# One layer on one core: experts on lists of the tokens that chose them, in place of every expert on every token

## The chip, the core and the metric

The kernel runs on one core of a Trainium2 chip. Its engines are TensorE (PE; PEld is its weight load), the vector engine (DVE), ScalarE (ACT), GpSimd (POOL) and SyncE (SP), which issues most transfers. Transfers between DRAM and the on-chip SBUF run on 16 DMA engines. The metric is device time in microseconds (us) of one execution; lower is better.

## What is computed

One layer on 4096 tokens of 256 features: a layer norm, causal attention with 16 heads of 16 features, a residual, a second norm, and a mixture of experts with a shared part. The expert part of the reference, cut:

```python
scores = sigmoid(xf @ gate_w.T); sfc = scores + gate_bias      # 16 experts in 4 groups
masked = where(in one of the 2 best groups, sfc, -inf)
_, topk_idx = top_k(masked, 4)                                  # 4 experts per token
topk_w = 2.5 * scores[topk_idx] / sum(scores[topk_idx])
cw = one_hot(topk_idx, 16) weighted by topk_w                   # 0 for the other 12
hg = einsum('nh,eih->nei', xf, Wg); hu = einsum('nh,eih->nei', xf, Wu)
y = einsum('nei,ne,ehi->nh', silu(hg) * hu, cw, Wd)             # i = 128
y = y + silu(xf @ Ws_g.T) * (xf @ Ws_u.T) @ Ws_d.T              # shared, 256 wide = 2 units
out = x + gb * (h + y)                                          # h: the normed input xf
```

Twelve of a token's sixteen expert weights `cw` are zero.

## The kernel before

All stages work on blocks of 512 tokens (8 blocks, `NB`). Every block of code ends in a barrier of all engines, after which the SBUF of its temporaries is given to the next.

- **prepare** (to 103 us): norm, transposes, queries, keys and values; parts of queries and keys go through DRAM.
- **attend** (to 1672 us): a list of events (`attention_order`) sets the order on every engine. POOL clears the triangle of each diagonal step (L628), and at 8 places adds the bias to a block of x (L618), which SP loads and stores (L606, L609).
- **project** (to 1777 us): a pipeline of 14 steps over the blocks. Per block PE projects the attention's result, DVE adds the residual (L980), takes statistics and normalises (L999), POOL raises to the power -0.5 (L942), PE transposes, ACT applies the modulation per feature and writes h2 (L914). A router chain on DVE (`router`, some 50 short instructions per two blocks) is threaded between. It makes `cw`, which goes to DRAM. Beside it SP loads the 18 units' weights (16 experts and the shared part as two units), ACT rounds each to float32r (`whi`, L909) and POOL takes the remainder (`wlo`, L945).
- **experts** (to 2404 us): each of the 8 blocks passes through all 18 units. A unit is 12 matmuls up (L1256: gate and up, two halves of the features, three products of high and low parts) and 6 matmuls down (L1267), all with 512 moving columns. ACT takes the silu (L1292) and the high part of the product (L1295), DVE multiplies by the up part (L1332), by `cw` (L1338) and takes the low part (L1345). The sum over the units stays in PSUM. Per block it is then scaled, turned back (L1278), added to x1 (L1363) and stored (L1233).

## Time and profile before

| | us |
|---|---|
| median of 3 runs | 2396.38 (2381.59 to 2401.0) |
| the profiled execution, its own time | 2405.99 |
| its span in the profile | 2404.3 |
| mean granted clock of TensorE, share of full | 0.947 |

The span is what the instructions cover; the execution's own time lies 1.7 us above it. A busy time is the time in which an engine executed; matmuls overlap, so the busy share of PE says less than the spacing of its instructions. An arrow names what the waiting instruction was released by.

### The profile page before, as it was taken

Reading aid. Unit: us, or ns where it says so; the run is one execution under the profiler, and the core shown is the slowest. Engines: PE = TensorE matmul, PEld = TensorE weight load, DVE = VectorE, ACT = ScalarE, POOL = GpSimd, SP = SyncE. Lnnn points to the kernel's source line nnn. Section 1 sums busy time; section 2 is a strip of 40 time slices with the busy share of each in tenths; the row PEclk is TensorE's granted clock in tenths of the full one; section 3 lists DMA queues with packets and bytes.
Section 4 is the critical chain, followed back from the end, with each engine's and each line's share of the span. In section 5 each row is a group of like instructions: output and inputs, shape, how many; then the busy total and the mean of one; then the engine's idle time right before and its main releaser. Section 6 shows DMA issues by size and latency. Waiting matters only on the chain. (4 is left out here: it accounts for less than half of the span.)

```text
span 2404.3 us, 42528 instructions
## 1 busy us (share of the span) xinstructions
PE 2245.1 (93%) x17842; PEld 1218.8 (51%) x17842; DVE 1756.9 (73%) x2243; ACT 1464.7 (61%) x2831; POOL 154.4 (6%) x191
## 2 busy tenths in 40 slices
PE   7689999999999999999999999998869999999998
PEld 5233333343444444444444333333758878788786
DVE  6478879999998878999998887762765555455554
ACT  5136657788888877788888888875523333333332
POOL 2000000000000011100000000000600000000000
PEclk9758969999999999999999999997969999999999
DMA  7715000004000003300000000001522221122211
GB/s 229 222 27 67 17 16 17 1 25 62 25 2 17 24 17 63 50 17 17 17 17 8 2 8 8 2 2 55 185 73 70 71 70 61 61 87 70 70 62 36
DMA packets 59907, 117.01 MB, mean 49 GB/s; under 512 B 7313, under 2 KB 20882, under 8 KB 58962
## 3 DMA queue, kind: packets, MB, share of 16 engines
q1 hardware_dynamic: 57168, 109.73, 16.7%
q10 hardware_dynamic: 2562, 4.77, 0.5%
q8 instruction: 129, 2.11, 0.4%
q14 instruction: 48, 0.39, 0.1%
HBM read 84.46 MB, written 29.62 MB: 47 GB/s over the span
## 5 line engine op out<-in xcount | busy, mean ns | idle before, releaser
L737 DVE TENSOR_REDUCE mx<-S 128x2 f32<-128x1024 f32 (+3 forms) x1152 | 1279.2, 1134 | 208.4 <-PE S L650 135.5
L718 ACT ACTIVATE prob<-ST 128x512 f32<-128x512 f32 (+3 forms) x2304 | 1168.6, 559 | 361.3 <-PE ST L671 316.5
L685 PE MATMUL O<-prob,V 128*17 128x256 f32 (+1 forms) x8704 | 691.0, 391 | 0.2 <-POOL prob L628 0.2
L650 PE MATMUL S<-K,Q 48*128 48x512 f32 (+3 forms) x2304 | 572.3, 495 | 33.0 <-DVE mx L737 23.1
L671 PE MATMUL ST<-Q,K 49*128 49x512 f32 (+3 forms) x2304 | 493.6, 425 | 36.3 <-ACT prob L718 30.7
L650 PEld LDWEIGHTS S<-K,Q 48*128 48x128 f32 x2304 | 224.5, 192 | 475.7 <-issue 293.5
L671 PEld LDWEIGHTS ST<-Q,K 49*128 49x128 f32 x2304 | 225.0, 191 | 138.3 <-ACT prob L718 105.7
L685 PEld LDWEIGHTS O<-prob,V 128*17 128x17 f32 x8704 | 145.7, 96 | 289.6 <-issue 280.3
L1295 ACT ACTIVATE ahi<-pr 128x512 fp32r<-128x512 f32 x144 | 91.1, 632 | 206.9 <-DVE pr L1338 194.8
L1292 ACT ACTIVATE sg<-hg 128x512 f32<-128x512 f32 x144 | 86.1, 598 | 209.2 <-PE hu L1256 208.5
L1332 DVE TENSOR_TENSOR sg<-sg,hu 128x512 f32<-128x512 f32 x128 | 88.0, 687 | 161.9 <-ACT sg L1292 161.3
L628 POOL TENSOR_SCALAR_AFFINE_SELECT prob<-prob 128x512 f32<-128x512 f32 x128 | 81.2, 635 | 1530.5 <-ACT prob L718 1530.5
L1345 DVE TENSOR_TENSOR alo<-pr,ahi 128x512 fp32r<-128x512 f32 x144 | 99.6, 692 | 100.5 <-ACT ahi L1295 100.5
L1267 PE MATMUL ya<-ahi,whi 128*128 128x512 f32 x288 | 113.3, 394 | 10.5 <-DVE alo L1345 10.5
L1256 PE MATMUL hg<-hhi,whi 128*128 128x512 f32 x288 | 114.0, 396 | 7.1 <-DVE hlo L1352 4.4
L1256 PE MATMUL hg<-hlo,whi 128*128 128x512 f32 x288 | 112.7, 391 | 0.0
L1256 PE MATMUL hg<-hhi,wlo 128*128 128x512 f32 x288 | 112.6, 391 | 0.0
L1256 PE MATMUL hu<-hhi,whi 128*128 128x512 f32 x288 | 112.5, 391 | 0.0
L1256 PE MATMUL hu<-hlo,whi 128*128 128x512 f32 x288 | 112.5, 391 | 0.0
L1256 PE MATMUL hu<-hhi,wlo 128*128 128x512 f32 x288 | 112.5, 391 | 0.0
L1267 PE MATMUL ya<-alo,whi 128*128 128x512 f32 x288 | 112.2, 389 | 0.0
L1267 PE MATMUL ya<-ahi,wlo 128*128 128x512 f32 x288 | 112.1, 389 | 0.0
(150 smaller groups left out, 1436.7 us busy)
## 6 DMA issues: line engine op xcount, KB each, us to landing
cwb<-cw SPq DMA_DIRECT2D x32, 1024.0 KB, 5.6
Q<-qs SPq DMA_DIRECT2D x192, 64.0 KB, 2.4
K<-ks SPq DMA_DIRECT2D x18, 512.0 KB, 15.3
qs<-hl SPq DMA_DIRECT2D x16, 512.0 KB, 4.4
ks<-hl SPq DMA_DIRECT2D x16, 512.0 KB, 4.2
wraw<-in_wcat SPq DMA_DIRECT2D x18, 384.0 KB, 3.4
xin<-in_x SPq DMA_DIRECT2D x4, 1024.0 KB, 12.5
xgate<-in_x SPq DMA_DIRECT2D x8, 512.0 KB, 3.8
```

The source lines that it names most:

```text
L628: pool.affine_select(out=tri, in_=tri, compare_op=ALU.is_ge, fill=0.0, base=0, pattern=[[0, HG], [1, P]], channel_multiplier=-1).then_inc( ...
L650: ins = pe.matmul(out[:, ab, 0:w], Q[g, n % QR, p, r * P:(r + 1) * P], K[G % 2][g, p, c * BW:c * BW + w], start=True, stop=not diag)
L671: pe.matmul(ST[(u + ab) % ST_BANKS][:, c0:BW], K[G % 2][g, p, k * P:(k + 1) * P], Q[g, n % QR, p, c0:BW], start=True, stop=True).then_inc( ...
L685: ins = pe.matmul(O[32 * a:32 * a + VC, c0:c1], V[:, G, k, VC * a:VC * (a + 1)], prob[:, s % NP, a, c0:c1], start=s in FIRST and h == 0, s ...
L718: act.activation(prob[:, s % NP, 2 * p + ab, c0:BW], ST[u % ST_BANKS][:, c0:BW], ACT.Exp).then_inc(s_exp, 1)
L737: dve.tensor_reduce(mx[:, n % 2, a:a + step + 1:step, c], S[slot % S_RING][:, :, 0:w], AX_X, ALU.max).then_inc(s_free, 1)
L1256: ins = pe.matmul(bank[:, :], w[:, u, c0:c0 + I], h[:, p, half, :], start=(m == 0), stop=(m == 5))
L1267: ins = pe.matmul(ya[p][:, half, :], w[:, u, c0:c0 + P], a[:, i, :], start=(u == 0 and m == 0), stop=(u == U - 1 and m == 2))
L1292: act.activation(sg[:, i, :], hg[i][:, :], ACT.Silu).then_inc(q["silu"], 1)
L1295: act.activation(ahi[:, i, :], pr[:, i, :], ACT.Copy).then_inc(q["ahi_done"], 1)
L1332: dve.tensor_tensor(sg[:, i, :], sg[:, i, :], hu[i][:, :], ALU.mult).then_inc(q["dve_chain"], 1)
L1345: dve.tensor_tensor(alo[:, i, :], pr[:, i, :], ahi[:, i, :], ALU.subtract).then_inc(q["act_full"], 1)
```

## The change

Each expert now gets a list of the tokens that chose it, in DRAM, and works on tiles of 512 rows of its list. The number of tiles is fixed at 47, which is (4096 x 4 + 16 x 511) / 512 rounded down, enough for any division of the tokens over the experts; which expert and which row a tile has is computed by the kernel and read into registers.

- **prepare**: the modulation of the second norm and the gate `gb` are made as rows spread over all partitions (`modB`, `gbB`), by four matmuls of 512 and 256 columns and DVE instructions of 128x256.
- **attend**: the bias of x leaves. In its place the weights are split: 54 pieces of 128x256 (3 per unit) are loaded (WL), on POOL rounded and the remainder taken, a third of them first scaled by `gbB` (WP), and both parts stored to DRAM (WS).
- **project**: x is loaded straight from the input, 6 blocks at first and 2 later, and POOL adds the bias (L953). DVE makes the modulated row h in two passes per tile of 128 tokens, into `xe`, which holds 256 features, the 16 weights and the token's number (273 columns). SP loads the split weights. After the router of two blocks, PE counts for every token and expert the earlier ones that chose it (`places`), DVE makes from it the row of the list (`placing`), and at the end `tiles` makes the tables of the tiles. POOL sends the first half of the 128 row groups to the lists (`scatter`).
- **experts**: POOL sends the other half. Meanwhile SP writes empty rows behind each list, clears the accumulator `acc1`, and the shared part runs on the 8 blocks with x1 and h added, into `acc0`. Then the 47 tiles: load the 512 rows, pick the weight of the tile's expert, turn, multiply up, multiply down with the tokens as output rows, scale by the weight, and add each 128 rows to `acc0` or `acc1` at their tokens' numbers (L1366 in the changed kernel). Last, `acc0` + `acc1` is the output.

The core of the diff:

```diff
+XW = D + E + 1
+CAP = T + BW
+NTILES = (T * TOPK + E * (BW - 1)) // BW
+SC_SPLIT = 2
+CWR = 4
+XR = 6
@@ attend, POOL
-                    if kind == "XS":
-                        need("xl", s_xl, 16 * (e + 1))
-                        pool.tensor_tensor(xg[:, :, :], xg[:, :, :], ...
+                    if kind == "WP":
+                        need("wl", s_wl, 16 * (e + 1))
+                        need("ws", s_ws, 32 * e)
+                        if e % 3 == 2:
+                            pool.tensor_tensor(wraw[:, :], wraw[:, :], t["gbB"][:, :], ALU.mult).then_inc(s_wp, 1)
+                            need("wp", s_wp, 3 * e + 1)
+                        pool.tensor_copy(wcut[:, 0, :], wraw[:, :]).then_inc(s_wp, 1 + (e % 3 < 2))
+                        need("wp", s_wp, 3 * e + 2)
+                        pool.tensor_tensor(wcut[:, 1, :], wraw[:, :], wcut[:, 0, :], ALU.subtract).then_inc(s_wp, 1)
@@ project, DVE
+                    for i in range(TPB):
+                        h = xe[:, TPB * b + i, 0:D]
+                        dve.scalar_tensor_tensor(out=h, in0=x_of(b)[:, i, :], scalar=mv[:, b % 2, i, 0:1],
+                                                 in1=t["modB"][:, 1, :], op0=ALU.subtract,
+                                                 op1=ALU.mult).then_inc(s_xm, 1)
+                        route(2)
...
+                        dve.scalar_tensor_tensor(out=h, in0=h, scalar=rstd[:, b % 2, i:i + 1],
+                                                 in1=t["modB"][:, 0, :], op0=ALU.mult, op1=ALU.add).then_inc(s_xn, 1)
@@ project, POOL, behind the last power(b)
+                for g in range(SC_SPLIT):
+                    pool.wait_ge(s_idx, g + 1)
+                    scatter(pool, t, d, g)
...
+def scatter(pool, t, d, g):
+    for n in range(2 * TPB * g, 2 * TPB * (g + 1)):
+        for k in range(TOPK):
+            pool.indirect_dma_start(d["lists"], bass.IndirectOffsetOnAxis(ap=t["rows"][:, n, k:k + 1], axis=0),
+                                    t["xe"][:, n, :], None).then_inc(t["s_sent"], 16)
@@ experts, SP
+                for b in range(2):
+                    load_block(b, x1(b))
+                need("pad", s_pad, 2)
...
+                for e in range(E):
+                    row = sp.value_load(t["pad_row"][0:1, e:e + 1], min_val=0, max_val=E * CAP)
+                    sp.dma_start(d["lists"][bass.ds(row, BW), :].rearrange("(i p) c -> p i c", p=P), fill
+                                 ).then_inc(s_pads, 16)
...
+                sp.dma_start(d["acc1"].rearrange("(i p) c -> p i c", p=P),
+                             pad[:, 0:D].unsqueeze(1).broadcast_to([P, NT + 1, D])).then_inc(s_pads, 16)
+                for b in range(NB):
+                    need("yb", s_yb, b + 1)
+                    sp.dma_start(rows_of(d["acc0"], b), xb[:, b % 2, :, :]).then_inc(s_xo[b % 2], 16)
+                    if b + 2 < NB:
+                        load_block(b + 2, x1(b + 2))
+                need("pads", s_pads, 16 * (E + 3))
+                need("sent", t["s_sent"], 16 * NT * TOPK)
+                for r in range(NTILES):
+                    need(f"xo{r % 2}", s_xo[r % 2], 16 * NB // 2)
+                    load_tile(r)
@@ experts, POOL
+                for g in range(SC_SPLIT, 4):
+                    scatter(pool, t, d, g)
...
+                for r in range(NTILES):
+                    need("cwt", s_cwt, r + 1)
+                    for i in range(TPB):
+                        need("y", s_y, TPB * r + i + 1)
+                        need(f"add{i % 2}", s_add[i % 2], 16 * (TPB // 2 * r + i // 2))
+                        pool.indirect_dma_start(
+                            d[f"acc{i % 2}"], bass.IndirectOffsetOnAxis(ap=idt[:, r % CWR, i:i + 1], axis=0),
+                            yo[:, r % 2, i, :], None, compute_op=ALU.add).then_inc(s_add[i % 2], 16)
@@ experts, ACT: scale(q), one tile behind
+                        need("d", s_d, ends[q])
...
+                        for i in range(2):
+                            need(f"add{i}", s_add[i], 16 * TPB // 2 * (r - 1))
+                        for i in range(TPB):
+                            act.activation(yo[:, r % 2, i, :], y[:, i, :], ACT.Copy,
+                                           scale=cwt[:, r % CWR, i:i + 1]).then_inc(s_y, 1)
```

The order that the change makes, at three places. On PE, in the experts' stage, a unit of a block was this (`hg`, `hu`: gate and up, `ya`: down; the rows for the second half of the features read the same):

```order
L1256 MATMUL hu<-hhi,whi 128x512
L1256 MATMUL hu<-hlo,whi 128x512
L1256 MATMUL hu<-hhi,wlo 128x512
L1267 MATMUL ya<-ahi,whi 128x512
L1267 MATMUL ya<-alo,whi 128x512
L1267 MATMUL ya<-ahi,wlo 128x512
L1256 MATMUL hg<-hhi,whi 128x512
```

The same place is now, for a tile (`wst`: the unit's weights copied by DVE, `tpe`: the turned rows of the tile after next, `ye`: down, tokens as output rows):

```order
L1416 MATMUL hu<-hhi,wst 128x512
L1403 TENSOR_LOAD tile_unit
L1403 ISA x2
L1383 MATMUL tpe<-identf,xs 128x128 x8
L1431 ISA
L1431 MATMUL ye<-whi,ahi 128x256
L1431 MATMUL ye<-whi,alo 128x256
L1431 REGISTER_ALU
L1431 MATMUL ye<-wlo,ahi 128x256
```

Twelve matmuls up stay as they were, six of 512 columns down became twelve of 256, and eight transposes and a read of a register per tile are new.

On DVE a tile of the experts' stage now has these rows:

```order
L1548 TENSOR_TENSOR sg<-sg,hu 128x512
L1550 TENSOR_TENSOR alo<-sg,ahi 128x512
L1509 SCALAR_TENSOR_TENSOR pick<-expert,tile_e,xs 128x64
L1513 CAST idt<-xs 128x4
L1515 TENSOR_REDUCE cwt<-pick 128x4
L1520 TENSOR_LOAD tile_unit
L1520 ISA x2
L1522 ISA
L1522 COPY wst<-whi 128x512
L1522 REGISTER_ALU
L1522 COPY wst<-wlo 128x512
L1526 TENSOR_TENSOR hlo<-tpe,hhi 128x512 x2
```

The multiplication by `cw` over 128x512 has left the unit; the split of the input (`hlo`), once per block before, and two copies of weights are in every tile.

On POOL the last instructions of the projection and those of the experts' stage are now these (a row with x64 stands for 64 transfers of 128 rows each):

```order
L949 TENSOR_TENSOR rstd<-ve,half 128x4 x4
L1215 DMA lists<-big,rows 74240x273 x64
L863 UNCONDITIONAL_BRANCH
L1350 UNCONDITIONAL_BRANCH
L1353 MEMSET pad 128x273
L1355 TENSOR_SCALAR pad<-token 128x1
L1215 DMA lists<-big,rows 74240x273 x64
L1366 DMA acc<-yo,idt 4224x256 x188
```

POOL had no instruction in the experts' stage; it now issues 64 transfers before the barrier at the projection's end and 64 + 188 behind it.

## Rows read from the trace of the kernel before

**Rows 1.** head of the page: span, busy us (share) and instructions by engine

```profile
span 2404.3 us, 42528 instructions
PE 2245.1 (93%) x17842; PEld 1218.8 (51%) x17842; DVE 1756.9 (73%) x2243; ACT 1464.7 (61%) x2831; POOL 154.4 (6%) x191
```

**Rows 2.** stretches: length, busy us (count) by engine, clock, DMA share, GB/s

```profile
0.00:103.00 103.00, 68.10 (x302) 42.19 (x302) 52.65 (x156) 41.82 (x82) 13.51 (x28) 0.92 0.85 258
103.00:1672.00 1569.00, 1501.22 (x14497) 617.56 (x14497) 1312.20 (x1281) 1185.66 (x2337) 100.00 (x137) 0.95 0.10 21
1672.00:1777.00 105.00, 72.39 (x388) 64.54 (x388) 76.36 (x350) 37.83 (x59) 40.92 (x27) 0.74 0.45 153
1777.00:2404.00 627.00, 603.35 (x2656) 494.52 (x2656) 315.73 (x456) 199.36 (x353) 0.00 (x0) 0.99 0.20 67
```

**Rows 3.** groups, projection and experts: count | busy us, mean ns | idle before

```profile
L1256 PE MATMUL hg<-hhi,whi 128*128 128x512 f32 x288 | 114.0, 396 | 7.1 <-DVE hlo L1352 4.4 <-issue 2.6
L1267 PE MATMUL ya<-ahi,whi 128*128 128x512 f32 x288 | 113.3, 394 | 10.5 <-DVE alo L1345 10.5
...
L1345 DVE TENSOR_TENSOR alo<-pr,ahi 128x512 fp32r<-128x512 f32 x144 | 99.6, 692 | 100.5 <-ACT ahi L1295 100.5
L1295 ACT ACTIVATE ahi<-pr 128x512 fp32r<-128x512 f32 x144 | 91.1, 632 | 206.9 <-DVE pr L1338 194.8 <-DVE pr L1341 12.1
...
L1332 DVE TENSOR_TENSOR sg<-sg,hu 128x512 f32<-128x512 f32 x128 | 88.0, 687 | 161.9 <-ACT sg L1292 161.3
L1292 ACT ACTIVATE sg<-hg 128x512 f32<-128x512 f32 x144 | 86.1, 598 | 209.2 <-PE hu L1256 208.5
...
L999 DVE TENSOR_SCALAR xn<-xres,mv,rstd 128x256 f32<-128x256 f32 x32 | 14.9, 502 | 0.0
...
L1352 DVE TENSOR_TENSOR hlo<-h,hhi 128x512 fp32r<-128x512 f32 x16 | 10.3, 685 | 3.6 <-ACT hhi L1304 3.6
...
L1363 DVE TENSOR_TENSOR x1b<-x1b,ya 128x1024 f32<-128x1024 f32 x8 | 9.7, 1214 | 3.4 <-PE ya L1278 3.4
...
L1044 DVE MAX8 top<-sfc 128x8 f32<-128x16 f32 x32 | 2.8, 161 | 0.1
```

**Rows 4.** order of time on PE, projection: start us, us, what, idle before

```profile
1740.07 1.04 PE L1098 MATMUL tpx<-identf,xn 128*128 128x128 f32 x8
...
1740.94 1.86 PE L1109 MATMUL gl<-gwT,h 128*128 128x16 f32 x16
```

**Rows 5.** transfers: out<-in, queue, count, KB each, median us from issue to landing

```profile
Q<-qs SPq DMA_DIRECT2D x192, 64.0 KB, 2.4
...
x1b<-x SPq DMA_DIRECT2D x8, 512.0 KB, 6.7
out<-x1b SPq DMA_DIRECT2D x8, 512.0 KB, 3.1
...
cw<-cwT ACTq DMA_DIRECT2D x4, 64.0 KB, 1.5
```

**Rows 6.** GpSimd's instructions: ns min/median/max, first and last start, forms

```profile
L618 POOL TENSOR_TENSOR xgate<-xgate,gab x8: 2362/2373/2379, 344.9 to 1241.0; 128x1024 f32<-128x1024 f32 x8
L945 POOL TENSOR_TENSOR wlo<-wraw,whi x18: 1795/1810/1928, 1689.5 to 1748.5; 128x768 fp32r<-128x768 f32 x18
L942 POOL TENSOR_TENSOR rstd<-ve,half x8: 1018/1246/1258, 1688.5 to 1745.7; 128x4 f32<-128x4 f32 x8
```

**Rows 7.** order of time: DVE beside POOL, and the projection's end

```profile
1745.70 1.11 POOL L942 TENSOR_TENSOR rstd<-ve,half 128x4 f32<-128x4 f32 x1 [4.97 <-DVE ve L992]
...
1746.78 3.55 POOL L945 TENSOR_TENSOR wlo<-wraw,whi 128x768 fp32r<-128x768 f32 x2
1746.80 1.82 DVE L1039 TENSOR_SCALAR gtmp<-gtmp 128x32 f32<-128x32 f32 x1
1748.53 1.95 DVE L999 TENSOR_SCALAR xn<-xres,mv,rstd 128x256 f32<-128x256 f32 x1
...
1751.35 0.40 DVE L999 TENSOR_SCALAR xn<-xres,mv,rstd 128x256 f32<-128x256 f32 x1
...
1774.66 0.39 DVE L1056 TENSOR_TENSOR cwe<-sc,wsum 128x128 f32<-128x128 f32 x1
...
1775.92 0.34 ACTq L905 DMA_DIRECT2D cw<-cwT  x1
...
1780.00 0.29 PEld L1256 LDWEIGHTS hg<-hhi,whi 128*128 128x128 f32 x1 [4.71 <-DVE hlo L1352]
```

**Rows 8.** groups on the vector engine, first stage: copies from PSUM and from SBUF

```profile
L250 DVE COPY gtmp<-modp 1x256 f32<-1x256 f32 x1 | 0.4, 414 | 0.0
...
L252 DVE COPY grow<-gtmp 1x256 f32<-1x256 f32 x1 | 0.3, 281 | 0.0
```

**Rows 9.** who waited for whom: us in total, times, longest us

```profile
POOL prob L628 <- ACT prob L718: 1530.5, 128, 94.1
```

More of the change, by code:

```diff
@@ L923, in _ @@
                         turned(k)
[L924 to L926 removed]
                     if 0 <= k - 3 < NB:
[L928 removed]
+                        normed(k - 3)
                     if k >= 5 and k % 2 and (k - 5) // 2 < 4:
                         sigmoid((k - 5) // 2)
[L931 to L933 removed]
@@ L1282, in _, with turn @@
-                run(pe, section)
+                need = needs(pe)
+                units = {}
+                def turn(q):
+                    kind, x = jobs[q]
+                    if kind == "R":
+                        need(f"xs{x % 2}", s_xs[x % 2], 16 * (x // 2 + 1))
+                    need("lo", s_lo, NS * q)
+                    for half in range(NS):
+                        for i in range(TPB):
+                            rows = xe[:, TPB * x + i, :] if kind == "S" else xs[:, x % 2, i, :]
+                            ins = pe.transpose(tp[:, half, i * P:(i + 1) * P], rows[:, half * P:(half + 1) * P],
+                                               t["identf"][:, :])
+                        ins.then_inc(s_tp, 1)
@@ new lines, in pick_unit, with up @@
+                def pick_unit(q):
+                    kind, r = jobs[q]
+                    if kind == "R":
+                        units[q] = pe.value_load(t["tile_unit"][0:1, r:r + 1], min_val=0, max_val=E)
+                def up(it):
+                    q, u, first, last = items[it]
+                    if first:
+                        need("lo", s_lo, NS * (q + 1))
+                    if u is None:
+                        need("wst", s_wst, 2 * (jobs[q][1] + 1))
+                    for k, bank in ((0, hg[it % 2]), (1, hu[it % 2])):
+                        m = 0
+                        for half in range(NS):
+                            c0 = (k * NS + half) * I
+                            for part, h in ((0, hhi), (0, hlo), (1, hhi)):
+                                ins = pe.matmul(bank[:, :], up_weights(part, it, c0), h[:, q % 2, half, :],
+                                                start=(m == 0), stop=(m == 5))
+                                m += 1
+                    ins.then_inc(s_u, 1)
@@ new lines, in down @@
+                def down(it):
+                    q, u, first, last = items[it]
+                    need("act", s_act, it + 1)
+                    if first and q:
+                        if jobs[q - 1][0] == "R":
+                            need("y", s_y, TPB * tiles_before(q))
+                        else:
+                            need("yb", s_yb, blocks_before(q))
+                    for i in range(TPB):
+                        for m, (a, part) in enumerate(((ahi, 0), (alo, 0), (ahi, 1))):
+                            ins = pe.matmul(y[:, i, :], a[:, it % 2, i * P:(i + 1) * P],
+                                            down_weights(part, it), start=first and m == 0 and i % 2 == 0,
+                                            stop=last and m == 2, skip_group_check=True)
+                    ins.then_inc(s_d, 1)
@@ new lines, in _ @@
+                high(0)
+                high(1)
+                for it, (q, u, first, last) in enumerate(items):
+                    need("u", s_u, it + 1)
+                    need("act", s_act, it - 1)
+                    act.activation(sg[:, it % 2, :], hg[it % 2][:, :], ACT.Silu).then_inc(s_sg, 1)
+                    need("pr", s_pr, it + 1)
+                    if it >= 2:
+                        need("d", s_d, it - 1)
+                    act.activation(ahi[:, it % 2, :], sg[:, it % 2, :], ACT.Copy).then_inc(s_ahi, 1)
+                    if last:
+                        for ahead in turned_after(q):
+                            high(ahead)
+                    if it and items[it - 1][3]:
+                        scale(items[it - 1][0])
@@ L1369, in build @@
+                for b in range(NB):
+                    need(f"xb{b % 2}", s_xb[b % 2], 16 * (NB // 2 + b // 2 + 1))
+                    need(f"sum{b % 2}", s_sum[b % 2], 16 * (b // 2 + 1))
+                    dve.tensor_tensor(xb[:, b % 2, :, :], xb[:, b % 2, :, :], yo[:, b % 2, :, :],
+                                      ALU.add).then_inc(s_yb, 1)
 def build(nc, d):
```

737 lines of the change are left out of this document (413 added, 324 removed).

## The prediction

> **What bounds the kernel now.** I read the head of the page, then the busy time by stretch, then the groups of the last two stages. TensorE is busy 93% of the span [rows 1]. In the experts' stage it is busy 603 of 627 us at a clock of 0.99, with DVE at 316 and ACT at 199 [rows 2], and DVE and ACT wait for PE and for one another while PE hardly waits [rows 3]. The 2656 matmuls there are 8 x 18 x 18 = 2592 plus 64 transposes [rows 2]. At 0.13 us for a transpose (8 in 1.04 [rows 4]) the 64 take 8 us, so one 512-column matmul costs (603 - 8) / 2592 = 0.229 us. The projection has nobody at its limit: PE 72 and DVE 76 of 105 us, clock 0.74 [rows 2]. The transfers reach their highest use in the first stage: 258 GB/s at a share of 0.85 [rows 2]. POOL is nearly idle, 154 us in all [rows 1].
>
> **What the change takes away.** 144 units of 18 matmuls become 16 shared units and 47 tiles, 63 in all. If PE stayed the bound, the stage would lose more than half. So the question is what else sets the pace, part by part. Sums are against the span, 2404.
>
> *Prepare, +3.* Four matmuls and some 13 DVE instructions of 256 columns, 0.28 to 0.41 us each [rows 8], about 4 us; the transfers beside them hide a part. Bounds 0 and +5.
>
> *Attend, 0.* POOL gets 54 x 2 + 18 instructions of 256 columns. At 1810 ns for 768 columns [rows 6] that is 0.6 us each, 76 us, against 19 us removed (8 x 2373 ns). Before its triangles POOL idles 1530 us waiting for ACT [rows 9], and the pieces stand behind each block's diagonal steps, so the idle time covers them. Without that cover, one piece delays one triangle by 1.2 us: bounds 0 and +10.
>
> *Projection, +25.* DVE works 76 us here. Per block, four normalising instructions (502 ns mean [rows 3], part of it spent beside POOL, see below) become eight with two inputs, 0.41 each: +1.3 us, and +0.1 of wait. Times 8: +11. `placing` adds per two blocks three short instructions, eight MAX8 (161 ns [rows 3]) and a wait for nine matmuls, 2.8 us: +11. `tiles` is 15 chained instructions of up to 752 columns, at 0.7 us per 512 columns [rows 3] for the large ones: +6. POOL holds DVE up less (8 x 2.4 us in place of 18 x 1.8 [rows 6]): -3. Bounds +12 (idle DVE absorbs half) and +35.
>
> *The first half of the scatters, +32.* They stand behind the last rstd, which starts at 1745.7; the last transfer of the stage is issued at 1775.9 [rows 7], 30 us later; with the additions above, about 48 us. The barrier waits for POOL. 64 transfers of 128 rows with an index each are something this trace doesn't have. From below: an issue on ACT's queue, 0.34 us [rows 7], so 22 us and nothing shows. From above: POOL's smallest instruction (1.25 us for four columns [rows 6]) plus such an issue, 1.6 us, so 103 - 48 = +55. I take 1.25, what POOL needs to start and end anything with arithmetic: 80 - 48 = +32. The end of the stage, so far DVE's router, becomes POOL's.
>
> *Shared part, 130.* A block on PE: 2 x (12 x 0.229 + 12 down of 256 columns) + 8 transposes. For 256 columns the bounds are 0.116 us (16 matmuls of 16 columns with a full weight load each in 1.86 us [rows 4], or half of 0.229) and 0.229; I take 0.13, a transpose's. That gives 2 x (2.75 + 1.6) + 1.04 = 9.7 us. But the load of x1 for the third block stands on SP's queue behind 17 writes of 0.56 MB and 4.3 MB of zeros, 13.8 MB. At 258 GB/s that is 54 us, and the POOL scatters take a share of the same engines: 62 us, plus a landing of 6.7 [rows 5]. DVE waits there for x1, and PE behind it. Then six blocks at 9.7 to 10.5: store 3.1, load 6.7 [rows 5] and an addition of 1.2 [rows 3] just fit a block. 68 + 62 = 130; bounds 90 and 165. The second half of the scatters (80 us) lies inside.
>
> *First tile, 23.* The last block's store 3.1 and the load 6.7 [rows 5], DVE's part 5.7 (below), and some 7 for PE and ACT one after the other with nothing beside.
>
> *47 tiles, 7.0 us each.* Three things can set the pace.
> PE: 2.75 + 1.6 + 1.04 = 5.4 us; at 0.229 per 256 columns, 6.5.
> DVE: 0.69 + 0.69 + 2 x 0.685 [rows 3], two copies of 512 columns at about 0.42 (281 ns for 256 from SBUF [rows 8]), three small ones 0.6, a register read (not in the trace; 0 to 1, taken as 0.8), a wait of 0.7 for the high part: 5.7, so about 5.9 with seams.
> The adds: POOL issues four per tile, alternately to two accumulators, and each waits until the one before it to the same accumulator has landed. So a tile takes two full round trips A. An adding transfer with indices is nowhere in this trace. From below: a 64 KB write, 1.5 us [rows 5], A hidden. From above: a read trip of 2.4, a write trip of 1.5 [rows 5] and POOL's 1.25 us [rows 6] in series, 5.2. In between, read and write trip with one of the two issues counted: 2.4 + 1.5 - 0.4 = 3.5. I take this, since the add must read the row and write it, and the descriptors can be followed while POOL still makes them. 2 x 3.5 = 7.0 us, above the other two. 47 x 7.0 = 329.
>
> *Last sum, 55.* 8 x 1.5 MB at 258 GB/s is 49 us, plus a landing.
>
> Experts' stage: 3 + 130 + 23 + 329 + 55 = 540 against 627, **-87**. In all -87 + 3 + 25 + 32 = **-27: 2377**. The profiled execution took 1.7 us more than its span, and 2406 is 0.4% above the median, 2396.4; so 2379 x 0.996 = **2370**, 1.1% under the median.
>
> **A rule against the change.** While POOL subtracted weights for 3.55 us, two DVE instructions with SBUF operands took 1.82 and 1.95 us, one of which takes 0.40 alone [rows 7]: the two engines shut each other out. In every tile DVE copies weights from SBUF to SBUF twice, and here it is POOL that would be late. The Trainium skill (SBUF — State Buffer, "SBUF: two separate sides") says that descriptors of a POOL transfer can't be written while DVE runs a two-port copy. The rows agree that there is such a lock, but show it with POOL in front; what it would do is a rival below.
> The same skill (DMA: Bandwidth & Descriptors, "Anatomy of one DMA — SWDGE (gpsimd) path") fits some 2.0 us plus bytes / 436 GB/s for a POOL transfer; as an estimate from that page an add of 128 KB takes 2.3 us, no row shows one, and by it the adds would be hidden, which is the first rival.
>
> **Rivals.**
> *Adds hidden.* If A stays under 2.95 us, DVE sets 5.9 us a tile: 47 x 1.1 = 52 less, 2325, times 0.996 and the 1.7: 2318. For it: small transfers land in 1.5 and 2.4 us. Against: the add holds a read and a write in series.
> *Adds slow (slower than before).* One round trip on one accumulator decides. At A = 4.5 us a tile takes 9.0: +94, 2463. From A = 3.8 on the gain is gone (94 x 0.3 = 28). PE would then idle over 3 us per tile; in the projection, with PE at 69% busy, the clock was 0.74 [rows 2], and at the lower level a tile costs PE 10.8 us, so it can't recover much. For it: 5.2 is the upper bound, and POOL's start alone is 1.25 us.
> *Copies shut POOL out.* Each of two copies of 0.42 us, and what is queued with it, delays one add of the chain by up to 0.7: 8.4 us a tile, +66, 2435.
> *The way to the first tile is longer.* Scatters at 1.6 us (+23) and a shared part of 160 us (+30): 2423. For it: 23 MB in 90 us is what the engines did at their fullest.
>
> **How the numbers follow.** The likeliest case, A from 2.95 to 3.8, spans about 2318 to 2398 and has 0.36. Adds hidden 0.21, slow adds 0.25, copies 0.08, longer way 0.10. About 1% is what a measurement of this kernel can tell from no change. Faster by over 1% (below 2372): all of adds hidden and 0.20 of the likeliest, 0.41. Within 1%: 0.15 of the likeliest and 0.03 of the last two, 0.18. Slower: 0.41. The range, 2295 to 2490, cuts a tenth on either side: below, A hidden and a projection and shared part at their lower bounds; above, A at 4.8. The likeliest case's own range is 2318 to 2398.
>
> **What would show it.** On the page of the changed kernel: POOL's transfers of the first scatter at 1.25 us each and running about 32 us past DVE's last table; PE idle at the third shared block for some 40 us, released by DVE behind x1; then a steady period of 7.0 us in the tiles, ACT's scaling released by an add's landing, spacing of adds to one accumulator 3.5 us; PE 5.4 us busy per tile. Tiles of 5.9 us with DVE full would show the first rival, a spacing of 4 us or more the second, adds longer only beside the copies the third. It is wrong altogether if the attention gets longer, since all else rests on it keeping 1569 us.

## The result and the profile after

The changed kernel takes 2621.9 us (median of 4 runs, 2613.9 to 2630.6) against 2398.7 us before (4 runs): a ratio of 1.093, with a 95% interval from 1.084 to 1.102. It is 9% slower, and 132 us above the upper end of the range. The profiled execution took 2620.9 us, its span is 2619.2. Rows of before are those of the groups ahead of the prediction.

By stage, in the profile of the changed kernel (busy time by stretch; columns as in [rows 2]):

```profile
0.00:103.00 103.00, 68.73 (x286) 42.04 (x286) 54.81 (x157) 41.77 (x82) 13.29 (x27) 0.93 0.84 255
103.00:1667.00 1564.00, 1496.81 (x14496) 618.18 (x14496) 1312.46 (x1281) 1186.65 (x2337) 154.99 (x254) 0.95 0.13 29
1667.00:1862.00 195.00, 91.20 (x458) 82.22 (x458) 101.81 (x458) 20.10 (x37) 93.58 (x92) 0.63 0.45 164
1862.00:2028.00 166.00, 90.77 (x448) 72.97 (x448) 59.85 (x73) 29.42 (x49) 63.92 (x66) 0.75 0.67 186
2028.00:2557.00 529.00, 320.57 (x1504) 280.13 (x1504) 188.59 (x423) 183.99 (x376) 297.61 (x187) 0.80 0.56 97
2557.00:2619.00 62.00, 0.00 (x0) 0.00 (x0) 9.80 (x8) 0.00 (x0) 1.56 (x1) 0.50 0.68 207
```

The stretches are prepare, attend, the projection, the shared part, the tiles and the last sum. The attention ends at 1667 us, as before (1672, [rows 2]). PE works 320 us in the tiles' 529 us, at a clock of 0.80 where [rows 2] have 0.99. The whole distance to the forecast lies between 1667 and 2557.

| | forecast | first profile | e9, the same kernel again (chip 12) |
|---|---|---|---|
| prepare and attend | 1675 | 1667 | 1677 |
| projection with the first scatters | 162 | 195 | 170 |
| shared part, to the first tile's load | 133 | 166 | 154 |
| first tile and 47 tiles, to the last add's issue | 352 | 529 | 523 |
| last sum | 55 | 62 | 60 |
| span | 2377 | 2619 | 2584 |

Two things stand out. The tiles carry 177 us of the 242. And the two stages beside the scatters have something in the first profile that isn't there in e9: the other engines crawl (below).

**The tiles.** Groups of the page (line, out<-in, count, busy and mean ns, idle time before and what ended it), which answer to [rows 3] and [rows 9]:

```profile
L1366 POOL DMA_INDIRECT acc<-yo,idt x188 | 299.2, 1591 | 313.5 <-DMA acc<-yo,idt 149.9
L1383 PE MATMUL tpe<-identf,xs 128*128 128x128 f32 x376 | 79.5, 382 | 186.8 <-DVE hlo L1526 180.3
L1509 DVE SCALAR_TENSOR_TENSOR pick<-expert,tile_e,xs 128x64 f32<-128x64 f32 x47 | 13.3, 284 | 247.8 <-DMA acc<-yo,idt 242.6
L1488 ACT ACTIVATE ahi<-sg 128x512 fp32r<-128x512 f32 x63 | 39.7, 631 | 196.3 <-DVE sg L1548 195.5
L1215 POOL DMA_INDIRECT lists<-big,rows x128 | 125.5, 980 | 38.9 <-issue 38.9
```

DVE waits 243 us for landings of adds, PE and ACT wait for DVE. POOL's timeline in the steady state (start, us, what, idle before and its releaser):

```profile
2300.56 1.56 POOL L1366 DMA_INDIRECT acc<-yo,idt  x1 [3.37 <-DMA acc<-yo,idt]
2302.42 1.56 POOL L1366 DMA_INDIRECT acc<-yo,idt  x1 [0.30 <-issue]
2305.04 1.70 POOL L1366 DMA_INDIRECT acc<-yo,idt  x1 [1.06 <-DMA acc<-yo,idt]
2307.04 1.56 POOL L1366 DMA_INDIRECT acc<-yo,idt  x1 [0.30 <-issue]
2311.25 1.56 POOL L1366 DMA_INDIRECT acc<-yo,idt  x1 [2.65 <-DMA acc<-yo,idt]
```

Every second add goes to the same accumulator. From 2300.56 to 2305.04 a round trip takes 4.5 us, from 2305.04 to 2311.25 it takes 6.2. Two trips make a tile: 10.7 us, where the forecast had 2 x 3.5. The longer one starts 0.8 us ahead of a tile's load of 546 KB; SP's queue in the same stretch (two loads' issues merged into one row):

```profile
2305.87 11.11 SPq L1310 DMA_DIRECT2D xs<-lists  x2
```

**The scatters.** They are issued every 1.27 us (0.97 and 0.30 of issue), as forecast. But beside them the other engines crawl: each issues its next instruction late, although nothing that the profile shows holds it. It begins some 20 us after the first scatter (1749.4). DVE's router chain in the first profile:

```profile
1782.63 0.18 DVE L1056 TENSOR_TENSOR grank<-grank,gtmp 128x16 f32<-128x16 f32 x1 [1.22 <-DVE gtmp L1055]
1784.03 0.18 DVE L1057 TENSOR_TENSOR grank<-grank,gtmp 128x16 f32<-128x16 f32 x1 [1.22 <-issue]
1785.43 0.17 DVE L1055 TENSOR_TENSOR gtmp<-gs 128x8 f32<-128x8 f32 x1 [1.22 <-DVE grank L1057]
...
1805.77 0.09 DVE L1068 MEMSET top<- 128x32 f32 x1 [9.69 <-issue]
```

Instructions of 0.18 us come 1.40 us apart, and one comes 9.7 us late with nothing to wait for. After the scatters the same chain runs at 0.21 us a step. In the shared part it is PE's turn:

```profile
1919.31 0.37 PE L1383 MATMUL tpe<-identf,big 128*128 128x128 f32 x1 [2.21 <-issue]
1922.11 0.37 PE L1383 MATMUL tpe<-identf,big 128*128 128x128 f32 x1 [2.43 <-issue]
1924.91 0.37 PE L1383 MATMUL tpe<-identf,big 128*128 128x128 f32 x1 [2.43 <-issue]
```

Eight transposes, which take 1.04 us in [rows 4], come one per 2.80 us here.

One more thing differs between the two profiles of this kernel. The view of transfers gives the time from issue to landing where the landings are on record. It has none for the scatters of the first profile, and 3.7 us in e9:

```profile
lists<-big,rows POOLq DMA_INDIRECT x128
```

```profile
lists<-big,rows POOLq DMA_INDIRECT x128, 3.7
```

From the first scatter until 10 us behind the last, the trace of the first profile holds 350 records of landings, that of e9 2463.

### The profile page after: what moved, and what is told of

Read it like the earlier page. It is cut to its first block and busy times, and to the rows that moved or that the text cites. A ratio compares the mean times of both kernels' runs of the same rounds, so it can differ in the third digit from the quotient of the medians.

```text
span 2619.2 us, 43281 instructions
## 1 busy us (share of the span) xinstructions
PE 2068.1 (79%) x17192; PEld 1095.5 (42%) x17192; DVE 1727.3 (66%) x2398; ACT 1461.9 (56%) x2881; POOL 624.9 (24%) x627
## 5 line engine op out<-in xcount | busy, mean ns | idle before, releaser
L1366 POOL DMA_INDIRECT acc<-yo,idt x188 | 299.2, 1591 | 313.5 <-DMA acc<-yo,idt 149.9
L1383 PE MATMUL tpe<-identf,xs 128*128 128x128 f32 x376 | 79.5, 382 | 186.8 <-DVE hlo L1526 180.3
L1383 PEld LDWEIGHTS tpe<-identf,xs 128*128 128x128 f32 x376 | 63.7, 198 | 204.6 <-issue 195.7
L1215 POOL DMA_INDIRECT lists<-big,rows x128 | 125.5, 980 | 38.9 <-issue 38.9
L1484 ACT ACTIVATE sg<-hg 128x512 f32<-128x512 f32 x63 | 37.7, 598 | 168.7 <-PE hu L1416 96.7
L1431 PE MATMUL ye<-whi,ahi 128*128 (+1 forms) x252 | 96.2, 382 | 33.5 <-DVE xs L1542 25.5
L1476 ACT ACTIVATE yo<-ye,cwt 128x256 f32<-128x256 f32 x188 | 73.8, 476 | 77.0 <-PE ye L1431 64.9
L1466 ACT ACTIVATE hhi<-tpe 128x512 fp32r<-128x512 f32 x110 | 63.3, 593 | 49.4 <-PE tpe L1383 46.4
L1431 PE MATMUL ye<-whi,alo 128*128 (+1 forms) x252 | 89.1, 353 | 2.0 <-issue 2.0
L1431 PE MATMUL ye<-wlo,ahi 128*128 (+1 forms) x252 | 88.1, 349 | 2.1 <-issue 2.1
```

The source lines that it names most:

```text
L1215: pool.indirect_dma_start(d["lists"], bass.IndirectOffsetOnAxis(ap=t["rows"][:, n, k:k + 1], axis=0), t["xe"][:, n, :], None).then_inc(t[" ...
L1366: pool.indirect_dma_start(d[f"acc{i % 2}"], bass.IndirectOffsetOnAxis(ap=idt[:, r % CWR, i:i + 1], axis=0), yo[:, r % 2, i, :], None, comp ...
L1383: ins = pe.transpose(tp[:, half, i * P:(i + 1) * P], rows[:, half * P:(half + 1) * P], t["identf"][:, :])
L1431: ins = pe.matmul(y[:, i, :], a[:, it % 2, i * P:(i + 1) * P], down_weights(part, it), start=first and m == 0 and i % 2 == 0, stop=last an ...
L1466: act.activation(hhi[:, q % 2, half, :], tp[:, half, :], ACT.Copy).then_inc(s_hi, 1)
L1476: act.activation(yo[:, r % 2, i, :], y[:, i, :], ACT.Copy, scale=cwt[:, r % CWR, i:i + 1]).then_inc(s_y, 1)
```

## The experiments

The theory from the profile: two chained round trips per tile set the pace. The rivals: a loop through the small tables that DVE makes per tile (`pick` waits for landings), DVE's copies, and the tile's load. And for the crawl: a backlog, the rate, the chip. Edits are against the changed kernel, and longer ones are shown by their core. A pace per tile is the mean spacing of ACT's first scaling of a tile over all 47; the changed kernel has 10.7 in the first profile and 10.6 in e9. Spans are compared stage by stage, since the attention alone ends between 1651 and 1696 us from run to run.

**e1, a tile's four adds to one accumulator.**

```diff
-                        need(f"add{i % 2}", s_add[i % 2], 16 * (TPB // 2 * r + i // 2))
-                            d[f"acc{i % 2}"], ...
+                    need(f"add{r % 2}", s_add[r % 2], 64 * (r // 2))
+                            d[f"acc{r % 2}"], ...
```

The waits of ACT and DVE for these landings follow the new order, and `acc0` and `acc1` get 512 spare rows for the empty rows; the diff leaves that out.

> The four adds of a tile go to the same accumulator, and tiles alternate between the two; a tile holds each token once, and the empty rows now have 512 numbers of their own, so the four needn't wait for one another, only for the tile before the last. Theory (chain of round trips: 4.5 + 6.2 us on one accumulator make the 10.7 us of a tile): POOL's issue sets the pace, 4 x (1.56 + 0.30) = 7.45 us per tile, 47 x 3.3 = 155 us less, span about 2464. Rival (the ring of the small tables and of yo, through which DVE and ACT wait for landings, sets the pace whatever the order of the adds): a tile stays over 10 us, span over 2590.

Measured: span 2479.2, 9.0 us per tile. POOL now does what the waits allow:

```profile
2211.75 1.67 POOL L1366 DMA_INDIRECT acc<-yo,idt  x1 [0.30 <-issue]
2213.73 1.56 POOL L1366 DMA_INDIRECT acc<-yo,idt  x1 [0.31 <-issue]
2218.67 1.55 POOL L1366 DMA_INDIRECT acc<-yo,idt  x1 [3.38 <-ACT yo L1475]
2220.53 1.56 POOL L1366 DMA_INDIRECT acc<-yo,idt  x1 [0.30 <-issue]
```

The chain was the first limit: without it 1.6 us per tile are gone. But half the forecast didn't come. After eight adds in a row POOL waits 3.4 us for ACT's scaling, and that stands behind DVE's `pick`, which waited for an earlier landing. Theory and rival were both half right, one behind the other.

**e10 and e11, deeper tables.** The ring of indices and weights is made 8 deep, alone (e10) and with e1's edit (e11).

```diff
-CWR = 4
+CWR = 8
```

> Only the ring of the small tables (indices and weights of a tile) is made 8 deep in place of 4, so that DVE's work for a tile waits for no landing of an add. Theory (the chain of trips on each accumulator sets the pace, DVE's wait only follows it): a tile stays at 10.4 us or more. Rival (the loop: landing, pick, product, down, scale, add sets the pace): a tile under 9.6 us, 50 us less.

> The tile's four adds on one accumulator as in e1, and the ring of small tables 8 deep as well. In e1 POOL issued eight adds in a row and then waited 3.4 to 3.8 us for ACT, behind DVE's wait for a landing: 9.07 us per tile in place of 7.45. Theory (two limits, one behind the other: first the chain, then the loop through the small tables, then POOL's issue): 7.45 to 7.6 us per tile, 47 x 1.55 = 73 us less than e1, span about 2410 without the crawl, 2450 with it. Rival (the ring of yo, two tiles, holds ACT back in the same way): 9.0 us as in e1.

Measured: e10 10.2 us per tile (its neighbour e9, the unchanged kernel, 10.6). e11 7.6 us, span 2436.4. POOL in e11:

```profile
2199.54 1.56 POOL L1366 DMA_INDIRECT acc<-yo,idt  x1 [0.30 <-issue]
2201.40 1.56 POOL L1366 DMA_INDIRECT acc<-yo,idt  x1 [0.30 <-issue]
2203.27 1.56 POOL L1366 DMA_INDIRECT acc<-yo,idt  x1 [0.30 <-ACT yo L1475]
2205.13 2.11 POOL L1366 DMA_INDIRECT acc<-yo,idt  x1 [0.30 <-issue]
```

The loop alone was worth 0.4 us, the chain alone 1.6, both together 3.0: they hid each other. What is left, 4 x 1.86 = 7.45 us, is POOL's own issue, now with hardly a gap.

**e2, plain writes in place of adds.** The sum over a token's experts is left out.

```diff
-                            yo[:, r % 2, i, :], None, compute_op=ALU.add).then_inc(s_add[i % 2], 16)
+                            yo[:, r % 2, i, :], None).then_inc(s_add[i % 2], 16)
```

> The adds of the tiles are plain indirect writes, with the same waits; the sum over a token's experts is left out by that. Theory (an add holds a read trip and a write trip in series): the round trip falls from 5.4 us on average to about 3, POOL needs 0.97 us for each as for the scatters, and DVE sets about 6 us per tile, 47 x 4.7 = 220 us less, span about 2400. Rival (the trip is POOL's own making of descriptors and the landing, the arithmetic costs nothing): trips stay over 4.5 us and a tile over 9.5 us, span over 2560.

Measured: span 2495.6, 8.5 us per tile. The loop held: DVE's tables still wait 113 us for landings.

```profile
DVE pick L1509 <- DMA acc<-yo,idt: 113.0, 42, 5.3
```

The trip itself:

```profile
2199.71 0.97 POOL L1366 DMA_INDIRECT acc<-yo,idt  x1 [2.89 <-DMA acc<-yo,idt]
2200.98 0.97 POOL L1366 DMA_INDIRECT acc<-yo,idt  x1 [0.30 <-ACT yo L1476]
2202.89 0.97 POOL L1366 DMA_INDIRECT acc<-yo,idt  x1 [0.94 <-DMA acc<-yo,idt]
```

3.2 us from issue to issue on one accumulator, 0.97 on POOL. So an add's trip, 4.5 us, is 1.3 us longer than a write's: 0.6 on POOL (1.56 - 0.97), 0.7 on the way. The trip was right (about 3), the pace was not: I had left the loop out.

**e3, no adds at all.** The experts' part doesn't reach the output.

> The adds of the tiles are left out, so the output lacks the 16 experts' part. What is left of a tile is PE, ACT, DVE and its load. Theory: 5.9 us per tile as in the prediction's sum for DVE, span about 2390. Rival (the seams between engines, with a clock at its lower level while PE waits, set more than DVE's work): 7 us or more, span 2440 or more.

Measured: span 2320.6, 5.5 us per tile. Busy time in ten such tiles, and for e11 in ten of its own:

```profile
2100.00:2155.00 55.00, 51.36 (x320) 44.15 (x319) 37.71 (x90) 36.76 (x80) 0.00 (x0) 1.00 0.36 103
```

```profile
2100.00:2176.00 76.00, 59.35 (x319) 49.19 (x318) 37.75 (x90) 36.74 (x80) 64.12 (x40) 0.91 0.81 143
```

PE works 5.14 of 5.5 us per tile, at full clock. The prediction's 5.4 for PE stands. Its 5.9 for DVE was too long, since DVE does all its work for a tile within the 5.5 too (of its terms, the register read was short: 0.55 us idle in place of the 0.8 taken). The rival, seams and a low clock, is out.

**e4 and e5, the two suspects for the longer trip.** e4 leaves the copies of the weights out, all tiles use unit 0. e5 loads only the first two tiles and works on them 47 times. Both change the experts' sum. (In e4 the copies and PE's wait for them go as well, in e5 two waits for the loads; the diffs leave that out.)

```diff
-                        return wst[:, q % 2, part, c0:c0 + I]
+                        return (whi, wlo)[part][:, 0, c0:c0 + I]
```

```diff
+                    if r >= 2:
+                        return
                     row = sp.value_load(t["tile_row"][0:1, r:r + 1], min_val=0, max_val=E * CAP)
```

> The two copies of a unit's weights per tile are left out; the up matmuls of every tile use unit 0, so the experts' part is another sum. Rival of the prediction (DVE's copies from SBUF to SBUF hold back the making of an add's descriptors, which makes the longer trip of 6.2 us): both trips 4.5 us, a tile 9.0 us, span about 2540. Theory (the longer trip comes from the tile's load, 546 KB, issued beside it): a tile stays at 10.5 to 10.8 us, span within 15 us of 2619.

> Only the first two tiles are loaded and their rows are used by all 47, so no transfer of 546 KB runs beside the adds; the experts' part is another sum. Theory (the tile's load beside the add makes the trip of 6.2 us): both trips about 4.5 us, a tile 9.0 us, span about 2540. Rival (the longer trip has another cause, DVE's copies or the adds' own overlap): a tile stays over 10.4 us.

Measured over all tiles from the 21st add on, from issue to issue where the landing released it: the trip beside the tile's load 6.3 us in the changed kernel (33 times in e9), 6.1 in e4 (28 times), 4.7 in e5 (3 times only, since the landing seldom came last there); the other trip 4.6, 4.5, 4.6. The pace: 10.6, 10.5 and 9.5 us per tile. Three trips are few, but e10 says the same: there the loads fall beside another add of the tile, and the longer trip moves with them. All 23 trips over 5.3 us had a load issued within them, of the 41 shorter ones 4. So the load of 546 KB lengthens an add that runs beside it by 1.6 us, and DVE's copies do next to nothing: POOL's issue beside them takes 1.70 in place of 1.56 us, the 1.70 in the timeline above, and 1.56 throughout in e4. e5 stays above twice 4.6 because POOL waits for ACT as well (38 of the last 168 adds), the loop again.

**e9 and e15, the changed kernel again.**

> The changed kernel as it is, once more. In its first profile and in two of the experiments since, the engines beside POOL crawl from some 20 us after the start of the scatters, with one instruction per 1.4 to 2.8 us; in the four experiments on one other chip they don't, with the same code in these stages. Theory (the crawl goes with the chip, or with how it was set up, and not with the kernel's edits): on a chip where it is absent here, the projection takes 167 us instead of 195 and the shared part 143 instead of 157, span about 2575; where it is present, 2620. Whichever it is, the kernels sent with this one show the same. Rival (it goes with the edits of the experiments): crawl here and none in the others.

> The changed kernel once more. On the chip of e1 to e4 and e9 to e12 the crawl beside the scatters was absent in eight of eight, on the chip of e5, e7 and e8 present wherever scatters ran. Theory (the chip, or its set-up, decides): with the crawl 2610 to 2630 and no landing times in the stretch of the scatters, without it 2575 to 2590; the four kernels sent together agree in that.

Measured: e9 ran on the chip of e1 to e4, span 2584.0, with no crawl. DVE at the same lines:

```profile
1789.39 0.18 DVE L1056 TENSOR_TENSOR grank<-grank,gtmp 128x16 f32<-128x16 f32 x1
1789.61 0.24 DVE L1057 TENSOR_TENSOR grank<-grank,gtmp 128x16 f32<-128x16 f32 x1
1789.88 0.17 DVE L1055 TENSOR_TENSOR gtmp<-gs 128x8 f32<-128x8 f32 x1
```

e15 ran on a third chip: span 2615.1, with the crawl. From the projection's start to DVE's last table it takes 128 to 130 us in e1 to e4 and e9 to e12, and 192 to 194 us in the first profile, e5, e8 and e15. So the edits don't decide it; it goes with the chip, or with how it was set up for that session. Chip 12 was free of it in two sessions; chips 10, 3 and 8, with one session each, all had it. Of the first profile the chip isn't on record.

It goes with the missing records of landings, too: in every profile with the crawl the scatters have no time to landing, in every one from chip 12 they have. e15 has 355 such records beside the scatters, like the first profile, against 2463 in e9. So what writes these records may be what is short, and the crawl may partly come from being recorded. No run was made to test that, and which of the two brings the other isn't shown. The crawl costs 25 us in the projection and 12 in the shared part (table above). The shared part without the crawl still waits, as forecast, for x1 of the third block behind the empty rows (e9; in the first profile PE waits only 15 us there, because the crawl had eaten the rest):

```profile
1935.70 0.55 PE L1431 MATMUL ye<-whi,ahi 128*128 128x256 f32 x1 [57.93 <-DVE xs L1542]
```

**e7 and e8, where the scatters stand.** None ahead of the barrier in e7, all in e8 (the same line with a 4).

```diff
-SC_SPLIT = 2
+SC_SPLIT = 0
```

> All 128 transfers of the scatters go after the barrier, none before. Theory (POOL's transfers hold back DVE's tables): the projection runs at the pace that it had until then and ends 100 + 25 = 125 us after its start, 70 us sooner; after the barrier POOL needs 162 us, so tiles can start no sooner than 165 us after it, and with the crawl at 190 or more. Span about 2619 - 70 + 20 = 2570. Rival (the late tables are DVE's own work): the projection keeps over 160 us, span over 2620.

> All 128 transfers go before the barrier. Theory: the projection's block ends with POOL, some 195 + 81 = 276 us long, and behind it the shared part runs without the crawl: SP's 23 MB at 250 GB/s take 92 us, so tiles start 100 to 110 us after the barrier in place of 175. Span about 2619 + 81 - 65 = 2635. Rival (the crawl comes from SP's empty rows and zeros, not from POOL's transfers): the shared part still takes 150 us or more with PE issuing one matmul per 1.4 to 2.8 us, span over 2680.

Measured on a chip with the crawl: e7, span 2637.7. The projection's tables are done after 129 us, near the 125 expected, but the span isn't the 2570 expected: the tiles' first load comes 241 us after the shared part's first silu (147 in e9; all times of the shared part from here on are measured so). During the 166 us of scatters PE got through one and a half blocks, and the rest came behind. e8, span 2630.4 (2635 expected): without scatters beside it the shared part takes 118 us and shows no crawl at all, with all of SP's empty rows in it. So the crawl comes with POOL's transfers, not with SP's alone. The total barely moves with the place, because on such chips much of the other engines' work and the scatters go one after the other.

**e12 and e16, at most four scatters in flight.**

```diff
+            if j >= 4:
+                pool.wait_ge(t["s_sent"][j % 4], 16 * (j // 4))
```

> Each transfer of the scatters waits until the fourth one before it has landed (at most four in flight, four semaphores in turn); nothing else changes. A landing took 2.5 us in a trace, so the waits should cost POOL nothing or up to 0.1 us each. Theory (the crawl is a backlog that builds up over some 16 transfers): with four in flight it is gone, the span falls by 40 us where the changed kernel shows it. Rival (it is the rate of the transfers, or the chip's own state): as in the changed kernel sent beside it, within 10 us in the stages before the tiles.

> The paced scatters of e12 once more. If the crawl shows in e15 here: theory (a backlog) no crawl, 40 us less before the tiles; rival (the rate, or the records kept of the transfers) crawl as in e15. If it doesn't show: as e12, the shared part 128 us against 147, since SP's transfers get a larger share of the engines.

Measured: e12 (no crawl there): the shared part 128 us against 147 in e9, since SP's transfers get through sooner, while the second half of the scatters takes 107 us in place of 82. e16, on the chip of e15: the projection's tables after 191 us, as in e15 (193), and the scatters there as close together as before, so the fourth one back had always landed. The crawl is no backlog of more than four transfers in flight. In the shared part, where the waits do space the scatters (111 us in place of 83), the crawl begins only some 80 us after the first of them, in place of 17 in the first profile: a sign that the rate counts.

**e13 and e14, everything mended.** e11, and zeros and the empty block's rows written in the projection, the experts' empty rows between the blocks of the shared part, 48 scatters ahead of the barrier, and (e13 alone) the last sum in pieces of 4 KB.

```diff
                     if b + 2 < NB:
                         load_block(b + 2, x1(b + 2))
+                    for e in range(2 + 3 * b, min(5 + 3 * b, E)):
+                        empty(e)
```

> e11 with three more changes. The empty row block, the zeros of acc1 and of acc0's spare rows go out at the end of the projection in place of the experts' stage; the 16 experts' empty rows go out between the blocks of the shared part, behind the load of the block's x1; 48 of the 128 scatters stand before the barrier in place of 64; the last sum moves 4 KB a partition in one piece in place of four rows of 1 KB. Theory: the projection ends 16 x 1.28 = 20 us sooner (148 us), POOL needs 80 x 1.28 = 103 us behind it, which the shared part (8 blocks of 10 us, its third no longer 50 us late) lies under: tiles start 110 to 115 us after the barrier in place of 147; tiles 7.6 us each as in e11; the last sum 45 us in place of 59. Span 2436 - 20 - 34 - 14 = 2368, 1% under the kernel before. Rival (the transfer engines are full in the shared part whatever SP's order, 26 MB at 250 GB/s): 135 us for it and span 2395 or more.

> As e13, but with the last sum as it was. Theory: 10 to 15 us more than e13, all of it behind the last add. Rival (the last sum is bound by the bytes, 12.6 MB, not by the pieces): within 4 us of e13 in that stretch.

Measured: 2463.8 us against 2390.2 before, ratio 1.033 (1.024 to 1.041), on a chip with the crawl, where 2368 had been expected. The tiles keep e11's 7.6 us. The shared part takes 180 us: the scatters end at 1928 and the tiles start at 2016, 88 us later, which is seven of the eight blocks, as PE had got through only one before. The last sum hardly cares about the pieces: from the last scaling to the end 69 us in e13, 72 in e14. e14's span, 2454.7, isn't above e13's 2458.2.

**e17 to e19, scatters further apart.** e17 is e13's kernel once more; the others have a memset of 256 (e19) or 512 columns (e18) on POOL behind each scatter, which does nothing but take time.

```diff
                                     t["xe"][:, n, :], None).then_inc(t["s_sent"], 16)
+            pool.memset(t["filler"][:, :], 0.0).then_inc(t["s_fill"], 1)
```

> The kernel of e13 once more. On a chip with the crawl: span 2450 to 2475. On one without it (theory of e13): projection 148 us, tiles start 110 to 115 us behind the barrier, span 2365 to 2385, under the kernel before or level with it.

> As e17, with a memset of 512 columns on POOL behind each scatter, so that they come about 1.9 us apart, as the adds do. Theory (the crawl hangs on the rate of the transfers; at the adds' pace of 1.86 us none was seen in the tiles): no crawl, DVE's tables 129 us after the projection's start in place of 174; the scatters take 128 x 1.9 = 243 us and set the start of the tiles, 320 us after the projection's start, against 365 in e13: 45 us less than e17 with the crawl, 75 us more than e17 without it. Rival (any stream of such transfers does it): crawl all the same, and 80 us more than e17.

> As e18 with a memset of 256 columns, about 1.65 us apart. Theory: between the two, the crawl begins later or not at all; scatters 211 us, tiles start 290 us after the projection's start without it. Rival: as for e18, 45 us more than e17.

Measured, all three on one chip: e17 2480.6 us (ratio 1.036, 1.024 to 1.048), with the crawl; e18 2412.8; e19 2391.6, the kernel before 2389.6. With more work on POOL the kernel takes 89 us less. e17 and e19 differ by 11 us in the attention already, which varies so from run to run (and e17's three runs lie between 2462.5 and 2495.2); from the attention's end to the tiles' first load it is 288 us in e19, 310 in e18 and 366 in e17, so 78 us are the spacing's. POOL in e19:

```profile
1760.10 0.97 POOL L1227 DMA_INDIRECT lists<-big,rows  x1 [0.17 <-issue]
1761.07 0.33 POOL L1231 MEMSET filler<- 128x256 f32 x1
1761.56 0.97 POOL L1227 DMA_INDIRECT lists<-big,rows  x1 [0.17 <-issue]
```

And PE's longest issue waits, first of e17, then of e19 (waited for: us in total, times, longest):

```profile
PE ye L1442 <- issue: 37.8, 8, 32.5
PE tpe L1394 <- issue: 19.9, 8, 3.1
```

```profile
PE gl L1199 <- issue: 9.6, 1, 9.6
PE pj L1165 <- issue: 2.0, 1, 2.0
```

1.46 us apart in place of 1.27 was enough to lose nearly all of the crawl; e18 came 1.67 us apart, not the 1.9 that I had reckoned with. The tables are done after 130 and 131 us instead of 173. The shared part takes 119 us in e19, 133 in e18 and 179 in e17; in e18 the scatters themselves set it. So the crawl hangs on the rate of these transfers. That fits the rival of the records as well, since every landing makes such records: beside the scatters e17 has 373 such records, e19 1779 and e18 2253. e19 stands level with the kernel before and not under it, by one run of it.

## Why the prediction was wrong

- **Prepare and attend, +3 and 0**: right, 1667 and 1677 against 1675. POOL's pieces took 74 us of the 76 forecast, hidden.
- **Projection, +25, and scatters, +32**: right where the crawl is absent, 170 against 162. A scatter costs 1.27 us against 1.25, and POOL does end the stage. With the crawl 195: nothing in the trace of before has such transfers, and I took the engines beside them to be free of them.
- **Shared part, 130**: 154 with the 3 of the barrier, inside its bounds of 90 to 165. The mechanism was right: PE waits at the third block, 58 us against "some 40". The step that was short is SP's writes beside the scatters, which get less than I gave them. e12 shows it by giving them more: the load of the third block is issued 68 us after the first one there, 84 in e9. Down matmuls of 256 columns come 0.12 us apart against 0.13 taken.
- **47 tiles, 7.0 us each: the step that failed.** The form of the sum was right, two full trips per tile, and so was that PE and DVE stay below it (both fit into e3's 5.5 us a tile). The size of the trip was not. I took A = 3.5, from "one of the two issues counted". Measured: 4.5 alone and 6.2 to 6.3 beside the tile's load, mean 5.4, over my upper bound of 5.2. Three things were wrong in it. It left POOL's start out and took one issue off, on the ground that the descriptors can be followed while POOL still makes them, for which it had no row; with POOL's start and nothing off it is 5.15, nearer to the 4.5 measured. The rows for the read and the write were of 64 KB, while an add moves 128. And the transfer of 546 KB that falls into every second trip wasn't in the bound at all. How the 4.5 us divide is shown only so far: 1.56 are POOL's, and 1.3 of the whole go with the adding (e2). 47 x 3.6 = 170 of the 207 us by which e9's span misses 2377.
- **Also missing**: the second loop, DVE's wait for landings before a tile's small tables. It cost little while the chain stood (0.4 us), and it would have taken half of the gain of any cure for the chain (e1).
- **The rivals**: *adds slow* was the one that came, beyond its own 4.5; it said 9.0 us a tile from A = 4.5, and with 5.4 its rule gives 10.8. Its chance, 0.25, was too low against 0.36 for the middle: the bound from above rested on three rows that add up in plain series, and that sum is nearer to what came (5.15 by rows, 4.5 measured) than the middle, 3.5. *Adds hidden* (A under 2.95) is out: even a plain write takes 3.2. *Copies shut POOL out* is out too: 0.14 us per tile (1.70 against 1.56), not 1.4. *A longer way to the first tile* came in part: in e9 projection and shared part are 29 us over the forecast, in the first profile 66, the rest by the crawl, which it didn't have.
- **The two rules.** Behind the rows on POOL's issue beside DVE's copies: the Trainium skill (SBUF — State Buffer, "SBUF: two separate sides") lets the copies hold descriptors back. The sign agrees (0.14 us), the size doesn't carry a term. Behind e2's trip: the same skill (DMA: Bandwidth & Descriptors, "Anatomy of one DMA — SWDGE (gpsimd) path") fits 2.0 us plus bytes / 436 GB/s, as an estimate 2.3 us for 128 KB. Measured are 2.5 us from a scatter's issue to its landing in the projection (the first row of e4's transfers below) and 8.0 beside SP's empty rows (the second), 3.2 from issue to issue for a chained plain write, and 4.5 for an add.

```profile
lists<-big,rows POOLq DMA_INDIRECT x59, 2.5
```

```profile
lists<-big,rows POOLq DMA_INDIRECT x54, 8.0
```

## What to carry to other kernels

A chain of dependent transfers costs its full round trip: before it is put into a loop, add its parts in series, take the sum and not a value inside the bounds, and look for the largest other transfer that falls into the same window. When one wait is taken away, look at once for the next loop through the same landings; here two of them alone were worth 0.4 and 1.6 us a tile, and together 3.0. And if engines wait for "issue" while another engine streams small transfers, try spacing the stream: here a slower producer made the kernel some 80 us faster. But first ask whether the crawl is there without a profiler, which this case leaves open.

## What the runs showed of the hardware

- An indirect transfer of 128 rows takes POOL 0.97 us (plain, rows of 1092 or of 1024 bytes) or 1.56 us (adding, 1024 bytes), and 0.30 more between two of them: 1.27 and 1.86 us apart.
- The round trip of an add of 128 rows of 1 KB is 4.5 us, of a plain write 3.2 us, and 546 KB loaded beside it add 1.6 us.
- A stream of such scatters 1.27 us apart made PE, ACT and DVE issue one instruction per 0.7 to 2.8 us, from 10 to 20 us after its start until up to 12 us behind its end, on three chips of four and in the first profile; SP's 16 empty-row writes were issued in 69 us in place of 46. Holding four in flight didn't help the projection, 1.46 us apart did. Adds 1.86 us apart did next to nothing (in e19's tiles DVE was late four times, 10.5 us in all; in e13's once, 2.4). What is short there is open. Wherever it shows, most records of landings beside the stream are missing, and every timed execution here was a recorded one, so the runs can't tell whether the recording takes part in it.
- PE, which worked 320 of 529 us in the tiles, had a mean clock of 0.80 there; without the adds, working 51.36 of 55, it had 1.00.
